# Starting a mixture-of-experts stage on half of a batch, with the other half's routing between expert tiles

## The reference

```python
# layer 0: x (4, 64, 64, 128); G=32 groups
x = x + _L0_conv_ref(_gn(x), ...)                  # 4-head attention over 4096 tokens of each batch
t = _to_tokens(x)                                  # (4, 4096, 128)
# layer 1: linear attention, whose output is normalised over a whole batch
t = t + _L1_attn_ref(_ln_t(t), ...)
#   out = out_proj(context @ q); (out - mean(batch)) * rsqrt(var(batch) + eps) * gn_w + gn_b
# mixture of experts: top 2 of 8, one 128x128 matrix for each expert
t = t + _L1_ffn_ref(_ln_t(t), ...)
#   p = softmax(x @ router_w + router_b); top_p, top_i = top_k(p, 2); top_p /= sum(top_p)
#   out = sum_k top_p[k] * (x @ expert_w[top_i[k]] + expert_b[top_i[k]])
```

## Time and profile before

| what | value |
|---|---|
| median of 3 runs | 3115.08 us (3114.53 to 3115.95) |
| the profiled execution: its time | 3113.02 us |
| its span, from the first to the last instruction | 3111.2 us |
| TensorE busy | 2907.3 us (93%) |
| VectorE busy | 2561.3 us (82%) |
| ScalarE busy | 2410.2 us (77%) |
| mean granted TensorE clock | 0.96 |

### The profile page before, as it was taken

The page is one execution under the profiler, slowest core; times in us unless marked ns, Lnnn a source line. Parts: engine busy times, 40 slices in busy tenths (PEclk is TensorE's granted clock), DMA queues, the critical chain, the costliest instruction groups (busy, mean ns, idle before and its releaser), DMA issues.

```text
span 3111.2 us, 62025 instructions
## 1 busy us (share of the span) xinstructions
PE 2907.3 (93%) x20374; PEld 1026.7 (33%) x20374; DVE 2561.3 (82%) x3575; ACT 2410.2 (77%) x3132; POOL 696.9 (22%) x726
## 2 busy tenths in 40 slices
PE   6999999988899999998979999999898999999988
PEld 3222222275322222237532222223743222222474
DVE  4888888878688888887868888888786888888877
ACT  4999999744599999974469999997446999999734
POOL 1122122114211222111421221221152222112115
PEclk8999999989899999999989999999898999999989
DMA  2555555500155555550025555554001556555400
GB/s 77 112 113 111 112 112 109 96 1 15 56 109 109 109 111 111 106 96 1 21 55 112 110 113 111 109 103 89 1 21 36 109 111 116 114 96 110 82 1 28
DMA packets 72164, 257.83 MB, mean 83 GB/s; under 512 B 8160, under 2 KB 10240, under 8 KB 71808
## 3 DMA queue, kind: packets, MB, share of 16 engines
q0 software_dynamic: 64512, 234.91, 40.0%
q1 hardware_dynamic: 7296, 18.51, 1.6%
HBM read 10.12 MB, written 8.39 MB: 6 GB/s over the span
## 4 chain that ended last, share of the span: by engine, by line
PE 78%; issue 10%; DVE 6%; DMA 2%; ACT 2%; POOL 1%; SPq 0%; ACTq 0%; DVEq 0%; POOLq 0%
PE BK L1070 77%; DMA RM<-EA 2%; DVE X L1041 2%; ACT KE L536 1%; POOL KE L459 1%; PE BK L1075 1%; ACT PVC L515 1%; DVE X L1033 0%; DVE ST L703 0%; ACT XT L545 0%; DMA WEXP<-in_L_ffn_expert_w 0%; DVE ST L647 0%; SPq L342 0%; DVE RU L640 0%; DVE RU L641 0%
## 5 line engine op out<-in xcount | busy, mean ns | idle before, releaser
L834 DVE TENSOR_TENSOR XT<-XT,KE 128x512 f32<-128x512 f32 x1344 | 1568.5, 1226 | 192.2 <-ACT KE L536 191.0
L536 ACT ACTIVATE KE<-BK 128x512 f32<-128x512 f32 (+1 forms) x1536 | 1488.9, 1021 | 151.8 <-PE BK L1070 64.8
L1070 PE MATMUL BK<-Q,K 32*128 32x512 f32 x8192 | 1191.2, 651 | 25.2 <-issue 12.9
L1070 PE MATMUL BK<-KE,V 128*32 128x512 f32 x6144 | 818.1, 606 | 0.0
L418 POOL DMA_DIRECT2D RM<-EA x448 | 391.9, 927 | 1541.4 <-ACT EA L536 726.4
L1070 PEld LDWEIGHTS BK<-Q,K 32*128 32x128 f32 x8192 | 326.1, 185 | 897.1 <-ACT KE L536 636.8
L536 ACT ACTIVATE EA<-BK 128x512 f32<-128x512 f32 (+1 forms) x512 | 496.9, 1025 | 34.7 <-PE BK L1070 6.5
L1070 PEld LDWEIGHTS BK<-KE,V 128*32 128x32 f32 x6144 | 125.5, 108 | 580.4 <-ACT KE L536 503.6
L1070 PE MATMUL BK<-EA,V 128*32 128x512 f32 x2048 | 272.7, 604 | 0.0
L1070 PE MATMUL BK<-WEXP,XT 128*128 128x512 f32 x512 | 239.7, 615 | 16.4 <-DVE X L1041 16.4
L615 ACT ACTIVATE RM<-BK,GT 128x128 f32<-128x128 f32 x512 | 145.6, 368 | 132.9 <-PE BK L1070 132.9
(11 more groups left out here) (167 smaller groups left out, 1841.8 us busy)
## 6 DMA issues: line engine op xcount, KB each, us to landing
RM<-EA POOLq DMA_DIRECT2D x224, 768.0 KB, 6.6
RM<-EA POOLq DMA_DIRECT2D x224, 256.0 KB, 3.3
XN<-in_x SPq DMA_DIRECT2D x16, 512.0 KB, 5.9
out<-X SPq DMA_DIRECT2D x16, 512.0 KB, 2.6
WEXP<-in_L_ffn_expert_w SPq DMA_DIRECT2D x1, 512.0 KB, 6.7
CONST<-in_consts SPq DMA_DIRECT2D x1, 384.0 KB, 5.6
WQKV<-in_L_conv_w_qkv SPq DMA_DIRECT2D x1, 192.0 KB, 2.4
WQKV<-in_L_attn_W_qkv SPq DMA_DIRECT2D x1, 192.0 KB, 6.0
```

What stands on the lines that cost most here:

```text
L536: nc.scalar.activation(exps(jt, p), scored(c * T + jt, p).rearrange("p a n -> p (a n)"), ACT.Exp, scale=SCALE0).then_inc(s_exp, 1)
L834: v.tensor_tensor(acc, acc, exps(jt, p), ALU.add).then_inc(s_adds, 1)
L1070: return nc.tensor.matmul(o, lhsT, rhs, start=start, stop=stop, skip_group_check=shared)
```

## The change

The residual is no longer added by VectorE in this stage. TensorE multiplies each chunk of X by the identity matrix into the chunk's bank, y2 is accumulated on top, and ScalarE copies the sum to X. Six of the eight identity products stand ahead of the wait for AT2. The two small matmuls of the norm use BK[7] in place of BK[0]. Only half 0 is routed fully before the experts. The chunks 5 to 7 of y2 and the transposes of half 1 follow the routing matmuls of half 0, then expert tile 0 begins. The routing matmuls of half 1 are spread over the expert tiles 3 to 6, four with each. On VectorE, statistics, deviations, logits and selection of half 1 move behind combine 0, 1 and 2.

```diff
@@ ScalarE
-                for c in range(NCH):
-                    transposed(1, c)
-                for half in range(2):
+                def onto_x(chunks):
+                    for c in chunks:
+                        act.wait_ge(s_y2, b * NCH + c + 1)
+                        part = X[:, c * TPB:(c + 1) * TPB, :].rearrange("p t c -> p (t c)")
+                        nc.scalar.activation(part, BK[c], ACT.Copy).then_inc(s_x1, 1)
+                def routed(half):
                     pr = PR[:, half * HALF:(half + 1) * HALF, :]
                     act.wait_ge(s_rt, b * 2 + half + 1)
                     nc.scalar.activation(pr, pr, ACT.Exp).then_inc(s_rte, 1)
+                onto_x(range(HCH))
+                for c in range(HCH):
+                    transposed(1, c)
+                onto_x(range(HCH, HCH + 1))
+                routed(0)
+                onto_x(range(HCH + 1, NCH))
+                for c in range(HCH, NCH):
+                    transposed(1, c)
                 for t in range(T):
+                    if t == 10:
+                        routed(1)
...
@@ VectorE
-                for c in range(HCH):
-                    onto_x(s_y2, s_x1, c)
                 half_statistics(0)
-                for c in range(HCH, NCH):
-                    onto_x(s_y2, s_x1, c)
                 deviations(mix_link, 0)
...
                 logits(0)
-                half_statistics(1)
                 probabilities(0)
                 pick(0, 2, OH)
                 second(0)
                 gates(0)
+                gates_out(0)
+                combine(0)
+                half_statistics(1)
+                combine(1)
                 deviations(mix_link, 1)
                 logits(1)
-                gates_out(0)
-                combine(0)
+                combine(2)
                 probabilities(1)
                 pick(1, 2, OH)
-                combine(1)
                 second(1)
-                combine(2)
                 gates(1)
                 gates_out(1)
                 combine(3)
@@ TensorE
+                def residual(c):
+                    part = X[:, c * TPB:(c + 1) * TPB, :].rearrange("p t c -> p (t c)")
+                    mm(BK[c], IDENT, part, stop=False, shared=True)
...
+                for c in range(NCH - 2):
+                    residual(c)
                 pe.wait_ge(s_at, b * 3 + 3)
+                # second(chunks): y2 of these chunks onto the residual (chunks 6 and 7 do theirs here)
+                # turned(chunks): transposes of X; route(half, places): routing matmuls
+                second(range(HCH))
+                turned(range(HCH))
+                second(range(HCH, HCH + 1))
+                pe.wait_ge(s_zc, b * (2 * NCH) + NCH + HCH)
+                route(0, range(HALF))
+                second(range(HCH + 1, NCH))
+                turned(range(HCH, NCH))
...
                 for t in range(T):
-                    if t == 1:
+                    if t == 2:
                         gates(0)
-                    if t == 2:
+                    if t == EBUF:
                         biases(0)
-                    if t == HALF - TPB + 1:
+                    if t == HALF - 2:
                         gates(1)
                     if t % TPB == 0 and t:
                         biases(t // TPB)
+                    if 0 < t < EBUF:
+                        pe.wait_ge(s_zc, b * (2 * NCH) + NCH + expert_banks(t)[-1] + 1)
+                    if t == EBUF:
+                        pe.wait_ge(s_zc, b * (2 * NCH) + 2 * NCH)
...
                     for part in range(2):
                         last = mm(expert_bank(t, part), ...)
+                        if part == 0 and EBUF <= t < EBUF + HALF // TPB:
+                            route(1, range(TPB * (t - EBUF), TPB * (t - EBUF) + 2))
                     last.then_inc(s_ex, 1)
+                    if EBUF <= t < EBUF + HALF // TPB:
+                        route(1, range(TPB * (t - EBUF) + 2, TPB * (t - EBUF) + 4))
```

More of the change, by code:

```diff
@@ L306, in hybrid_kernel, with expert_banks @@
         PAIRS = T // 2 * 3
+        def expert_banks(t):
+            return 1 + 2 * (t % EBUF), 2 + 2 * (t % EBUF)
         def expert_bank(t, part):
-            return BK[1 + 2 * (t % EBUF) + part]
+            return BK[expert_banks(t)[part]]
         def exps(jt, p):
@@ L940, in _ @@
                 dve.wait_ge(s_gst, b * 2 + 1)
-                mix_link(v.tensor_copy(SMALL[:, 0:1], BK[0][:, 0:1]))
+                mix_link(v.tensor_copy(SMALL[:, 0:1], BK[7][:, 0:1]))
                 mix_link(v.tensor_tensor(SMALL[:, 1:2], MV[:, 0:1], SMALL[:, 0:1], ALU.add))
@@ L945, in _ @@
                 dve.wait_ge(s_gst, b * 2 + 2)
-                mix_link(v.tensor_scalar(RA[:, 0:1], BK[0][:, 1:2], -1.0, 1e-5, ALU.mult, ALU.add))
+                mix_link(v.tensor_scalar(RA[:, 0:1], BK[7][:, 1:2], -1.0, 1e-5, ALU.mult, ALU.add))
                 rsqrt(mix_link, SMALL[:, 3:4], RA[:, 0:1], 1)
@@ L1313, in _, with second, turned, route @@
                 pe.wait_ge(s_bst, b * 2 + 1)
-                mm(BK[0][:, 0:1], NEG, MV[:, 0:1]).then_inc(s_gst, 1)
+                mm(BK[7][:, 0:1], NEG, MV[:, 0:1]).then_inc(s_gst, 1)
                 pe.wait_ge(s_bst, b * 2 + 2)
-                mm(BK[0][:, 1:2], NEG, SMALL[:, 2:3]).then_inc(s_gst, 1)
+                mm(BK[7][:, 1:2], NEG, SMALL[:, 2:3]).then_inc(s_gst, 1)
+                for c in range(NCH - 2):
+                    residual(c)
                 pe.wait_ge(s_at, b * 3 + 3)
-                tiles(lambda t: QT[:, t * P:(t + 1) * P], lambda t: AT2[:, :], s_y2)
-                for half in range(2):
-                    for c in range(half * HCH, (half + 1) * HCH):
+                def second(chunks):
+                    for c in chunks:
+                        if c >= NCH - 2:
+                            residual(c)
+                        for t in range(c * TPB, (c + 1) * TPB):
+                            last = mm(BK[c][:, (t % TPB) * C:(t % TPB + 1) * C], QT[:, t * P:(t + 1) * P], AT2[:, :],
+                                      start=False, shared=True)
+                        last.then_inc(s_y2, 1)
+                def turned(chunks):
+                    for c in chunks:
                         pe.wait_ge(s_x1, b * NCH + c + 1)
                         transposes(BK[c], lambda t: X[:, t, :], c).then_inc(s_zT, 1)
-                    pe.wait_ge(s_zc, b * (2 * NCH) + NCH + (half + 1) * HCH)
-                    for i in range(HALF):
+                def route(half, places):
+                    for i in places:
                         t = half * HALF + i
                         last = mm(BK[7 * half][:, i * EXPERTS:(i + 1) * EXPERTS], XT[:, t * P:(t + 1) * P], WR[:, :])
-                    last.then_inc(s_route, 1)
+                    if places[-1] == HALF - 1:
+                        last.then_inc(s_route, 1)
+                second(range(HCH))
[5 more added lines that the diff above has]
+                turned(range(HCH, NCH))
                 def gates(half):
```

## The result

The changed kernel took 3146.49 us, the median of 4 runs (3144.67 to 3147.63); the kernel before took 3114.81 beside it (3112.74 to 3115.95). The ratio is 1.0103, interval 1.009 to 1.0115: 31.7 us slower. The forecast was 3156, 41 slower. The profiled execution took 3144.67 with a span of 3142.8, 31.6 more than the span before.

A forecast was written before the change was run, and what follows sets the result against it. VectorE and TensorE wait in turn up to the first combine, VectorE limits until the gates of half 1, then TensorE. 20 us from steps 1 to 5 plus 21 for the clock: 3113 + 41 + 2 = 3156 us, range 3121 to 3176.

The forecast's parts named there:

- Steps 1 to 3: Stage head: routing of half 0 ends at 16.5, its gates ready at 24.6, first bias add at 31.6 us.
- step 2: Routing to gates of half 0: statistics of half 1 gone from here, gates ready at 24.6, 7.3 us earlier.
- step 1: Up to the routing of half 0: it ends at 16.5, 4.5 us earlier than before.
- Rival (c): Experts begin no earlier, held by half-clock identity products and ScalarE's queue: 10.3 us lost a batch, 3156; chance 0.05.
- Step 4: First bias add to gates of half 1: 7.6 us of VectorE work moved in; gates 3.9 us later.
- The GpSimd term: VectorE's moved instructions held up beside GpSimd's adds: 1.6 us a batch, between 0.5 and 3.
- Step 5: Gates of half 1 to biases 4: half clock in every batch, 7.2 us; mean change +1.1 a batch.
- Step 6: Tiles 3 to 7: half clock after a 2.8 us wait costs 9 us in two or three batches, 21 in all.
- (a): Clock holds in tiles 3 to 7 because the wait is short enough: +20, 3135 us; chance 0.20.
- (b): Faster, as VectorE's moved work fits into waits: -2.9 us a batch, 3103 us; chance 0.06.
- step 3: Up to the first combine: first bias add at 31.6, 6.6 us earlier, at best 9, at worst 3.
- (d): Half clock in tiles 3 to 13 in all batches, from each bank wait: +75, 3190 us; chance 0.04.

The follow-up runs named there:

- b_late_half_only: The changed kernel with y2 added to X by VectorE again and no identity products; 3150.11 us, ratio 1.0115 against the kernel before.
- the pair of light kernels: The changed kernel and the kernel before, each with GpSimd's three adds cut to one column of each tile; 3115.1 and 3096.07 us.
- f_filler: The changed kernel with three unused 512-column products in TensorE's 2.5 us wait before tile 3; 3137.98 us, ratio 1.0073.
- l_filler_before_gates: The changed kernel with half 1's norm, routing, logits and selection moved forward, gates copied by ScalarE, four unused products before the gates of half 1; 3099.63 us.
- g_route_block: The changed kernel with the routing of half 1 in one piece ahead of tile 3, not spread over tiles 3 to 6; 3139.23 us, ratio 1.0082.
- d_gpsimd_light: The changed kernel with GpSimd's three adds cut to one column of each tile; 3115.1 us, ratio 0.9997 against the kernel before.

## Why the prediction was right, and where its sum was off

**Steps 1 to 3** closed: 16.9 for 16.5, 25.1 for 24.6, 31.3 for 31.6. The first bias add came 7.3 earlier on the mean, where 6.6 had been charged; 0.4 of the difference is that batch 0 of before, from which it was reckoned, is the earlier kind. (Three slips in the working change nothing: step 2 starts from 16.6 where step 1 ends at 16.5, the 1.76 of an expert tile is two products in four records and not four products, and 2.4 x 9 is 21.6.) Rival (c), no earlier start, fell with this mark. What brings the earlier start is the order on TensorE, since `b_late_half_only` has it without the identity products.

**Step 4** had the right mechanism: work moved into the stretch in which VectorE is the limit costs more than the earlier start brings. The stretch grew by 14.8, of which 7.6 is the moved work. The GpSimd term was too small: 1.6 was charged, and the pair of light kernels measures 13 us over four batches, 3.3 a batch, above the upper bound of 3 (what follows from it, tile 11 at half clock among it, is in the 3.3). The deviations alone grew by 3.2 in batch 0. The bound came from one overlapped instruction; not counted was that the deviations are sixteen in a chain, and that three adds for each pair of tiles come by. With the clock's 2.1 (`f_filler`), 14.8 - 7.6 - 3.3 - 2.1 leaves 1.8, for the 1.3 charged for TensorE's routing pieces. That rest was not measured by itself, but VectorE's idle time bears it out: in `f_filler` it is 5.0, of which 2.4 was there before and 1.1 is the wait for tile 11, and 1.5 is left.

**Step 5** was charged at +1.1 and measured +0.3. The wait before the gates of half 1 was 4.8 to 5.6 (5 was forecast), and half clock followed in all four batches, as forecast: their transposes took 1.11 or 1.12 in each, not 0.66. From gates 1 to biases 4 it took 6.1 or 6.8, where 7.2 was reckoned.

**Step 6** is the term that was mis-sized, and it was the largest. Half clock came in tiles 3 to 7 in all four batches, at the place named and behind a wait of 2.51 (2.8 was forecast). But it was reckoned at 9 us in two or three batches, 21 in all. It lasted 3 to 7 us, and `f_filler` measures 8.5 over all four. The mistake was the price from batch 1 of before, where the whole routing ran dear: here the clock was back before tile 4 began. There was also a loss that the prediction did not name: the held-up deviations made TensorE wait 5.43 before tile 11, not 2.16, tile 11 ran at half clock, and VectorE waited 1.11 a batch for it (counted under GpSimd above).

The terms against what was measured, over four batches: the earlier start -2.8, GpSimd +6.8, the rest of step 4 +2.0, step 5 -3.2, step 6 -12.6. That is -9.8, and 41 - 9.8 = 31.2, the four times 7.8 of the marks; it closes because the rest of step 4 was taken as what was left. That the forecast came within 10 us is in part luck: with GpSimd and the rest of step 4 charged as measured the sum would have been 49.8, and 18.6 too high.

**The other rivals.** (a), the clock holds, is refuted by the windows, though its price was good: `f_filler`, in which the clock does hold there, took 3138.0 against its 3135. (b), faster, asked for a gain in step 3 above 7.6 plus what GpSimd holds up; it was 7.3, and GpSimd held up 3.3. (d), half clock from tile 3 to 13 everywhere, is refuted by the 1.00 of 721 to 741. The rule that the prediction weighed (the Trainium skill, "TensorE: Matmul & The Clock Gate", section "A second HAM failure mode: psum-queue depth-cycling") agrees with this trace in that the clock fell behind waits of 2.51 and more in every batch, and not in the way the prediction carried it over, that any cycling through banks would do: it was 1.00 behind 1.75 us, and in `l_filler_before_gates` the tile behind a wait of 1.75 took the full-clock 1.98 in every batch.

## What to carry to other kernels

Starting a stage earlier by moving a chain of small instructions into it pays only if the start gained is more than the moved work plus what that work now runs beside; here 7.3 us a batch were gained and 7.6 moved, before any side effect. Before moving work, look at what runs beside its new place: on VectorE a chain of small instructions next to GpSimd's adds took twice its time here. Where a tuned stage has a wait on TensorE that cannot be removed, matmuls that nobody reads can hold the clock, and one experiment with them tells what the clock is worth. Here a stretch at half clock cost half its length; what overstated it was a length taken from another batch of another order.

## What the runs showed of the hardware

- An instruction with one SBUF input was held up beside GpSimd: the 128x16 `tensor_scalar` at 733.78 took 1.16 us, not 0.17. The Trainium skill ("SBUF — State Buffer", section "Who interferes with whom") exempts instructions with at most one SBUF input only outside the 2-port modes, which this row agrees with if it ran in one; no row shows the mode.
- The clock also fell with TensorE never idle, behind matmuls of 8 columns: in `g_route_block` the tile right behind 4.19 us of them took 3.76, not 1.98. Behind 2.74 us of unused products of 512 columns, in the same place, the clock was 1.00. So useful work in a wait and work that holds the clock are two things.
- How long a wait the clock survives is not one number here: behind 2.51 us it fell in all four batches of the changed kernel and of `d_gpsimd_light`, behind 2.16 in one of four of the latter; behind 2.65 in one batch of four of the kernel before (from gates 1 to biases 4 it took 7.4 there, 5.7 in the others).
- Holding the clock was cheap: 14 us of unused products over the run (four times 3.60) in a wait, and 9.0 us gained.
